# Slot experts of a ViT tower: a new queue order for the expert loads, a wait per part, and late fetches beside the last groups

## The chip, the cores and the metric

One core of a Trainium2 chip runs the whole kernel in one launch. The metric is the device time of that launch in microseconds (us), lower is better. The chip's other cores run nothing. The time before is the median of three runs; a profile of one further execution was taken by the hardware profiler.

## The reference

Input: 32 images of 96x96x3, cut into 36 patches of 16x16, plus a class token: 37 tokens of 192 per image. All arithmetic in the part that matters here is float32. Four stages follow each other, each with a residual and a layer norm:

1. low-rank attention with 12 heads;
2. a soft mixture of experts with 64 slots (the stage that is changed);
3. differential attention with 12 heads (two maps, `out1 - exp(lambda) * out2`), projected by `Wo`;
4. a segmented MLP with top-4 gates.

Stage 2, cut to what is computed:

```python
logits = einsum('sd,btd->bst', slot_directions, tokens)
dispatch_w = softmax(logits, axis=-1)
combine_w = softmax(logits, axis=-2)
y = einsum('btd,bst->bsd', xn, dispatch_w)               # 64 slot inputs per image
y = gelu(einsum('sio,bsi->bso', fc1_weight, y) + fc1_bias)   # 64 experts, 192 -> 768
y = einsum('sio,bsi->bso', fc2_weight, y) + fc2_bias         # 64 experts, 768 -> 192
out = einsum('bsd,bst->btd', y, combine_w)
```

Each of the 64 slots has its own two weight matrices, 192x768 and 768x192, so this stage reads 75 MB of weights, and each is used for 32 rows only.

## The kernel before

The kernel is written engine by engine. Each engine runs its own list of instructions in the order written, and waits for semaphores that others raise. There is no scheduler.

**Expert stage.** The 64 slots go in 16 groups of 4 (`GROUPS`, `GS`). A group needs `fc1` in three transfers: `fc1_tall` (128 partitions x 3072 words, 1536 KB), `fc1_short` (128 x 1536, 768 KB) and `fc1_b` (4 x 768, the bias, 12 KB); and `fc2` in two: 128 x 4608 words (2304 KB) and `fc2_b` (3 KB). All lie in one SBUF tile, `stream`, in two slots each (even and odd groups). The profile writes `fc1` and `fc2` alike as `in_fc_dram`.

**PE, `moe_pe` (L724).** `first(g)` makes the hidden layer of group g: 2 bias products (L728), 8 products with the tall part (L733), 8 with the short part (L739). A float32 product is two or more records in the trace, so that the counts there are twice these. Ahead of it stands one wait for 48 on `s_fc1`, which all three transfers of the group raise by 16 each; L733 also waits for the slot inputs that ACT stages (L775, L778). When `first(g)` is done, `s_hid` rises, and ACT applies gelu (L784). `second(g)` transposes the hidden layer (L747, 6), DVE copies it to SBUF (L799), PE adds the bias (L752) and makes 24 products with `fc2` (L757), and `s_fo` rises; DVE copies the result to `y_out` (L804) and raises `s_yo`. The order on PE is first(0), then first(1), second(0), first(2), second(1), first(3), second(2) and so on, to first(15), second(14), second(15).

**SP, `moe_sync` (L687).** SP issues the loads. Groups 0 and 1 are loaded during stage 1. Then a loop over pairs of groups, unrolled twice, in this order for each group g: wait until first(g-2) is done, issue the three transfers of fc1(g); wait until second(g-2) is done, issue fc2(g) and its bias; wait for `y_out`, store the 96 KB of group g-2 to `y_dram` (L689). Behind the loop come the stores of groups 14 and 15, the four weight matrices of stage 3 (L706, 864 KB together), and, when all stores have landed, the fetch of all slot outputs from `y_dram` into `y2` (L710, 2 transfers of 768 KB, in runs of 768 bytes). PE begins stage 3 (`l1_pe`, L898) when the four matrices and both halves of `y2` are there; its first products are those of L859.

**POOL, `split_pool` (L806),** works at the same time: it loads the first MLP weights, splits them into three bf16 parts and stores them (L822, L825).

Names that the change touches: `k_heads1` and the four late matrices share `stream` with the expert weights (L131, L133); `load_fc1` (L672), `moe_sync_first` (L681), `moe_sync` (L687), `first` (L725), the last three calls of `moe_pe` (L767 to L769), the wait at L899.

Of the kernel before, what the change touches and what calls it, by code (L numbers as in the profile page):

```python
# [22 lines left out]
SLOTS = 64  # L23
# [25 lines left out]
def tower(nc, io):  # L49
# [23 lines left out]
    with ExitStack() as ctx:  # L73
# [57 lines left out]
        k_heads1 = tenant(stream, FH, 0, [2, 2, QB, HH, T])  # L131
        w1s = tenant(stream, ZR, W1_AT, [SEG, SM * SH], bf16)
        late = Tenants(stream, KH * 2)  # L133
# [474 lines left out]
        s_fc1 = [sem("s_fc1_even"), sem("s_fc1_odd")]  # L608
        s_fc2 = [sem("s_fc2_even"), sem("s_fc2_odd")]
# [62 lines left out]
        def load_fc1(sp, u, g):  # L672


            w = io["fc1"][g]
            sp.dma_start(fc1_tall[:, u], w[0:64].rearrange("r k j h -> (r k) j h")).then_inc(s_fc1[u], 16)
            sp.dma_start(fc1_short[:, u],
                         w[64:FH].rearrange("r k (a j) h -> (r k a) j h", a=2)).then_inc(s_fc1[u], 16)
            sp.dma_start(fc1_b[:, u, :], w[FH:FH + 1, 0].rearrange("o j h -> (o j) h")).then_inc(s_fc1[u], 16)

        def moe_sync_first(sp):  # L681
            for g in range(2):
                load_fc1(sp, g, g)
                sp.dma_start(fc2[:, g], io["fc2"][g]).then_inc(s_fc2[g], 16)
                sp.dma_start(fc2_b[:, g, :], io["fc2_b"][g]).then_inc(s_fc2[g], 16)

        def moe_sync(sp):  # L687
            def store(g, u):
                sp.dma_start(y_dram.rearrange("s b d -> (s b) d")[ds(g * 128, 128), :], y_out[:, u, :]).then_inc(s_yd[u], 16)  # L689

            with sp.Fori(1, GROUPS // 2) as it:
                for u in range(2):

                    sp.wait_ge(s_hid, it * 2 + (u - 1))
                    load_fc1(sp, u, it * 2 + u)
                    sp.wait_ge(s_fo, it * 2 + (u - 1))
                    sp.dma_start(fc2[:, u], io["fc2"][it * 2 + u]).then_inc(s_fc2[u], 16)
                    sp.dma_start(fc2_b[:, u, :], io["fc2_b"][it * 2 + u]).then_inc(s_fc2[u], 16)
                    sp.wait_ge(s_yo, it * 2 + (u - 1))
                    store(it * 2 + (u - 2), u)  # L700
            for g in (GROUPS - 2, GROUPS - 1):
                sp.wait_ge(s_yo, g + 1)
                store(g, g % 2)

            for dst, name in ((w_q1, "w_q1"), (w_k1, "w_k1"), (w_v1, "w_v1"), (w_o1, "w_o1")):
                sp.dma_start(dst, io[name]).then_inc(s_late, 16)  # L706
            for u in range(2):
                sp.wait_ge(s_yd[u], 16 + 16 * (GROUPS // 2))
            for e in range(2):
                sp.dma_start(y2[64 * e:64 * e + SLOTS, :, :],  # L710
                             y_dram.rearrange("s (p e) d -> e s p d", e=2)[e]).then_inc(s_y2, 16)
# [12 lines left out]
        def moe_pe(pe):  # L724
            def first(it, u):  # L725
                pe.wait_ge(s_fc1[u], nth(it, 48, 48))
# [3 lines left out]
                pe.wait_ge(s_yr, nth(it, 6, 3 * u + 3))  # L730
                for n in range(2):
                    for j in range(GS):
                        pe.matmul(P[32 * j:32 * j + B, 2 * u + n, 0:HID // 2], tall_ring[:, u, B * j:B * (j + 1)],  # L733
                                  fc1_tall[:, u, j, n * (HID // 2):(n + 1) * (HID // 2)],
                                  start=False, stop=False, skip_group_check=True)
                for n in range(2):
# [25 lines left out]
            with pe.Fori(0, GROUPS // 2 - 1) as it:  # L762
# [3 lines left out]
                second(it, 1)  # L766
            first(GROUPS // 2 - 1, 1)  # L767
            second(GROUPS // 2 - 1, 0)
# [86 lines left out]
        def l1_pe(pe):  # L855
# [43 lines left out]
            pe.wait_ge(s_y2, 32)  # L899
# [904 lines left out]
```

## Time and profile before

| | |
|---|---|
| median of 3 runs | 1058.68 us (1057.67 to 1059.81) |
| the profiled execution, own time | 1055.97 us |
| its span in the profile | 1054.2 us |
| mean granted clock of TensorE | 0.819 of full |
| PE busy | 810.4 us (77%) |
| DVE busy | 562.6 us (53%) |
| ACT busy | 367.6 us (35%) |
| moved by DMA | 102.56 MB |
| transfers of expert weights on the chain of waits, by the page | 8% of the span |

The span is what the profiler saw of the program's work, so it is a little shorter than the execution's own time. The profile names instructions by line and tile: "L757 PE MATMUL P<-stream,work" is line 757 on PE, writing PSUM from `stream` and `work`. "SPq" is SP's queue issuing a transfer. The granted clock is a share of TensorE's full 2.4 GHz; 0.50 is 1.2 GHz. The DMA share is the mean busy share of the core's 16 DMA engines; since packets overlap it can read a little above 1.

### The profile page before, as it was taken

How to read it: one execution, taken by the hardware profiler on the slowest of the kernel's cores; microseconds unless marked ns; L12 is line 12 of the kernel's file. 1: busy time of each engine (PE TensorE's matmuls, PEld its weight loads, DVE VectorE, ACT ScalarE, POOL GpSimd, SP SyncE). 2: the span in 40 equal slices, each digit the busy share in tenths (PEclk: the TensorE clock that was granted, in tenths of full speed). 3: DMA queues.
4: the chain of work that ended last, by engine and by line, in shares of the span. 5: the costliest groups of instructions: out<-in, count | busy, mean ns of one | idle time of the engine just before them, and what ended most of it. 6: DMA issues, size and time to landing. Idle time of an engine off the chain costs nothing.

```text
span 1054.2 us, 19852 instructions
## 1 busy us (share of the span) xinstructions
PE 810.4 (77%) x6882; PEld 460.3 (44%) x6882; DVE 562.6 (53%) x1563; ACT 367.6 (35%) x785; POOL 98.4 (9%) x133
## 2 busy tenths in 40 slices
PE   6899999668677777729998897542799899899930
PEld 4567777553233333316766665211333333233310
DVE  4455656530000000025676867888587588677850
ACT  0313222203111111103334333233587587677700
POOL 0020201012322000000010110133000000000010
PEclk9786959558778788868898989665699999989975
DMA  8410000006999888686000000452200000000000
GB/s 311 188 36 1 35 0 0 1 1 218 373 387 405 338 354 356 270 160 84 1 2 1 0 1 1 139 80 44 60 2 1 2 1 1 2 1 1 1 13 23
DMA packets 24822, 102.56 MB, mean 97 GB/s; under 512 B 3359, under 2 KB 14563, under 8 KB 20531
## 3 DMA queue, kind: packets, MB, share of 16 engines
q1 hardware_dynamic: 23702, 98.37, 27.6%
q0 software_dynamic: 1056, 3.44, 1.0%
q8 instruction: 27, 0.44, 0.2%
q14 instruction: 37, 0.30, 0.1%
HBM read 93.08 MB, written 5.07 MB: 93 GB/s over the span
## 4 chain that ended last, share of the span: by engine, by line
PE 62%; DVE 14%; DMA 11%; issue 6%; SPq 2%; ACT 2%; POOL 1%; DVEq 0%; ACTq 0%; POOLq 0%
DMA stream<-in_fc_dram 8%; PE P L1440 7%; PE P L1415 7%; PE P L1424 7%; PE P L353 6%; PE P L1089 5%; PE P L415 4%; PE P L388 3%; PE P L399 3%; PE P L728 2%; PE P L733 2%; PE P L739 2%; PE P L757 2%; PE P L370 2%; PE P L1433 2%
## 5 line engine op out<-in xcount | busy, mean ns | idle before, releaser
L1584 DVE TENSOR_TENSOR work<-work,P 128x396 f32<-128x396 f32 x384 | 193.1, 562 | 65.3 <-PE P L1424 45.3
L1511 ACT ACTIVATE work<-P 128x396 f32<-128x396 f32 x384 | 178.5, 500 | 57.3 <-PE P L1415 56.9
L1415 PE MATMUL P<-stream 99*128 x384 | 129.4, 340 | 12.1 <-ACT work L1511 10.4
L1424 PE MATMUL P<-early,middle 96*128 x384 | 129.8, 339 | 0.6 <-DVE work L1584 0.6
L799 DVE COPY work<-P 128x768 f32<-128x768 f32 x16 | 15.3, 958 | 160.1 <-PE P L747 160.1
L1440 PE MATMUL P<-work 128*32 128x396 f32 x768 | 84.6, 508 | 0.0
L1415 PEld LDWEIGHTS P<-stream 99*128 99x128 bf16 x384 | 37.8, 98 | 100.5 <-ACT work L1511 54.2
L784 ACT ACTIVATE work<-P 128x768 f32<-128x768 f32 x16 | 13.0, 811 | 173.1 <-PE P L739 173.1
L728 PE MATMUL P<-stream,slot_sel 4*128 4x384 f32 x64 | 34.7, 676 | 47.3 <-DMA stream<-in_fc_dram 47.3
L584 POOL TENSOR_SCALAR work<-work 101x4 f32<-101x4 f32 x16 | 3.7, 229 | 700.0 <-DVE work L574 700.0
L1089 PE MATMUL P<-early 128*37 128x192 f32 x384 | 53.9, 361 | 10.1 <-DMA early<-in_patches_dram 7.1
L490 ACT ACTIVATE work<-work 101x444 f32<-101x444 f32 x48 | 28.1, 586 | 95.6 <-DVE work L485 95.6
L415 PE MATMUL P<-work 101*37 101x34 f32 x1152 | 53.9, 227 | 2.8 <-DVE work L474 2.8
L399 PE MATMUL P<-ident,work 101*128 101x101 f32 x288 | 44.5, 303 | 15.0 <-ACT work L490 12.5
L1424 PEld LDWEIGHTS P<-early,middle 96*128 96x128 bf16 x384 | 37.8, 98 | 35.4 <-DVE work L1584 17.4
L415 PEld LDWEIGHTS P<-work 101*37 101x37 f32 x1152 | 49.1, 142 | 9.5 <-issue 6.8
L1089 PEld LDWEIGHTS P<-early 128*37 128x37 f32 x384 | 37.0, 126 | 26.0 <-issue 10.5
L399 PEld LDWEIGHTS P<-ident,work 101*128 101x128 f32 x288 | 33.3, 169 | 34.2 <-issue 18.1
L353 PE MATMUL P<-work,stream 96*96 96x296 f32 x128 | 41.0, 484 | 4.1 <-DVE work L949 3.5
L757 PE MATMUL P<-stream,work 128*32 128x192 f32 x768 | 34.5, 328 | 8.5 <-DVE work L799 8.5
L457 DVE TENSOR_SCALAR stream<-P,hmask 96x296 f32<-96x296 f32 x48 | 21.5, 514 | 36.6 <-PE P L353 36.6
L480 DVE TENSOR_REDUCE work<-P 101x12 f32<-101x444 f32 x48 | 29.6, 616 | 21.0 <-PE P L388 20.7
(210 smaller groups left out, 1208.0 us busy)
## 6 DMA issues: line engine op xcount, KB each, us to landing
stream<-in_fc_dram SPq DMA_DIRECT2D x16, 2304.0 KB
stream<-in_fc_dram SPq DMA_DIRECT2D x16, 1536.0 KB
stream<-in_fc_dram SPq DMA_DIRECT2D x16, 768.0 KB
early<-stream SPq DMA_DIRECT2D x36, 99.0 KB, 2.3
early<-in_patches_dram SPq DMA_DIRECT2D x4, 888.0 KB, 5.1
stream<-w_dram SPq DMA_DIRECT2D x6, 512.0 KB
work<-in_w_dram SPq DMA_DIRECT2D x1, 2048.0 KB, 8.2
stream<-z_dram SPq DMA_DIRECT2D x6, 297.0 KB, 10.0
```

The costliest lines, as they stand in the source:

```text
L353: mm = pe.matmul(P[0:FH, at + mc, 0:QT], w[:, kc, m * D + mc * FH:m * D + (mc + 1) * FH], h_t[:, kc, :, :], start=(kc == 0), stop=(kc == 1))
L388: mm = pe.matmul(P[64 * e:64 * e + T, u % 2, mc * HH * T:(mc + 1) * HH * T], q_t[:, m, mc, b * T:(b + 1) * T], k_heads[:, m, mc, b, :, :], ...
L399: mm = pe.transpose(P[:, 4 + 2 * (u % 2) + hp // 3, (hp % 3) * ROWS:(hp % 3 + 1) * ROWS], probs[0:ROWS, u % 2, hp, :, :].rearrange("p a k ...
L415: mm = pe.matmul(P[64 * e:64 * e + T, 2 + u % 2, hp * w2:(hp + 1) * w2], probs_t[0:ROWS, u % 2, hp, 64 * e:64 * e + T], v_blk[0:ROWS, 2 * ...
L728: pe.matmul(P[:, 2 * u + n, 0:HID // 2], slot_sel[:, :], fc1_b[:, u, n * (HID // 2):(n + 1) * (HID // 2)], start=True, stop=False, skip_gr ...
L757: mm = pe.matmul(P[32 * j:32 * j + B, 6 + u, 0:D], hidden_t[:, u, c, B * j:B * (j + 1)], fc2[:, u, c, j, :], start=False, stop=(c == HC - ...
L1089: mm = pe.matmul(P[64 * e:64 * e + T, 2 + j // 2, (j % 2) * D:(j % 2 + 1) * D], patches[:, c, 2 * j + e, :], w_patch[:, c, :], start=(c == ...
L1415: pe.matmul(P[:, n % 3, 0:TC], w1s[:, seg, i * 128:(i + 1) * 128], zs[:, seg, ds(it * TC, TC)], start=True, stop=True).then_inc(s_u1, 1)
L1424: pe.matmul(P[:, 3 + n % 3, 0:TC], gate_sel[:, c, :], ws[:, 2 * seg + hh, ds(it * TC, TC)], start=True, stop=True).then_inc(s_bc, 1)
L1440: pe.matmul(P[32 * j:32 * j + 32, 6 + sq, 0:TC], w2[:, i, seg, :], gated[:, n % 8, :], start=False, stop=(hh == 1 and c == CH // 2 - 1), s ...
L1511: act.activation(act_out[:, n % 4, :], P[:, n % 3, 0:TC], ACT.Gelu_apprx_tanh).then_inc(s_ua, 1)
L1584: dve.tensor_tensor(gated[:, n % 8, :], act_out[:, n % 4, :], P[:, 3 + n % 3, 0:TC], ALU.mult).then_inc(s_ug, 1)
```

## The change

Four things:

1. SP issues each load when its own buffer comes free. `first(g-1)` ends on PE ahead of `second(g-2)`, so fc1(g+1) now stands ahead of fc2(g) in SP's list, where it stood behind it. The loop is written out (no registers). The store of a group moves with its fc2 step.
2. The bias parts are issued first of their group, and fc1's three transfers have a semaphore each; PE waits for each part just ahead of the products that read it.
3. PE's last three calls become second(14), first(15), second(15).
4. The four late matrices and `k_heads1` change places in `stream`, so that the matrices lie in the even slot of `fc1_tall`, free after first(14). They are issued behind fc2(15), with 12 of 16 groups' slot outputs (48 of 64 slots); the stores of groups 14 and 15 and a fetch of the last 16 slots follow. PE waits for four transfers of `y2` where it waited for two.

```diff
-        k_heads1 = tenant(stream, FH, 0, [2, 2, QB, HH, T])
+        k_heads1 = tenant(stream, FH, 12 * D, [2, 2, QB, HH, T])
...
-        late = Tenants(stream, KH * 2)
+        late = Tenants(stream)
...
             w = io["fc1"][g]
+            sp.dma_start(fc1_b[:, u, :], ...).then_inc(s_fc1_b[u], 16)
             sp.dma_start(fc1_tall[:, u], w[0:64]...).then_inc(s_fc1[u], 16)
-            sp.dma_start(fc1_short[:, u], ...).then_inc(s_fc1[u], 16)
-            sp.dma_start(fc1_b[:, u, :], ...).then_inc(s_fc1[u], 16)
+            sp.dma_start(fc1_short[:, u], ...).then_inc(s_fc1_short[u], 16)
+
+        def load_fc2(sp, u, g):
+            sp.dma_start(fc2_b[:, u, :], io["fc2_b"][g]).then_inc(s_fc2[u], 16)
+            sp.dma_start(fc2[:, u], io["fc2"][g]).then_inc(s_fc2[u], 16)
...
         def moe_sync(sp):
-            with sp.Fori(1, GROUPS // 2) as it:
-                for u in range(2):
-                    sp.wait_ge(s_hid, it * 2 + (u - 1))
-                    load_fc1(sp, u, it * 2 + u)
-                    sp.wait_ge(s_fo, it * 2 + (u - 1))
-                    sp.dma_start(fc2[:, u], ...).then_inc(s_fc2[u], 16)
-                    sp.dma_start(fc2_b[:, u, :], ...).then_inc(s_fc2[u], 16)
-                    sp.wait_ge(s_yo, it * 2 + (u - 1))
-                    store(it * 2 + (u - 2), u)
-            for g in (GROUPS - 2, GROUPS - 1):
-                sp.wait_ge(s_yo, g + 1)
-                store(g, g % 2)
+            def gather(groups, at, to):
+                for u in range(2):
+                    sp.wait_ge(s_yd[u], 16 + 16 * (groups // 2))
+                for e in range(2):
+                    sp.dma_start(y2[64 * e + at:64 * e + to, :, :],
+                                 y_dram.rearrange("s (p e) d -> e s p d", e=2)[e, at:to]).then_inc(s_y2, 16)
+
+            for g in range(2, GROUPS + 1):
+                if g < GROUPS:
+                    sp.wait_ge(s_hid, g - 1)
+                    load_fc1(sp, g % 2, g)
+                if g > 2:
+                    sp.wait_ge(s_fo, g - 2)
+                    load_fc2(sp, (g - 1) % 2, g - 1)
+                    store(g - 3)
+
+            sp.wait_ge(s_hid, GROUPS - 1)
             for dst, name in ((w_q1, "w_q1"), (w_k1, "w_k1"), (w_v1, "w_v1"), (w_o1, "w_o1")):
                 sp.dma_start(dst, io[name]).then_inc(s_late, 16)
-            for u in range(2):
-                sp.wait_ge(s_yd[u], 16 + 16 * (GROUPS // 2))
-            for e in range(2):
-                sp.dma_start(y2[64 * e:64 * e + SLOTS, :, :], ...).then_inc(s_y2, 16)
+            gather(GROUPS - 4, 0, SLOTS - 4 * GS)
+            for g in (GROUPS - 2, GROUPS - 1):
+                store(g)
+            gather(GROUPS, SLOTS - 4 * GS, SLOTS)
...
             def first(it, u):
-                pe.wait_ge(s_fc1[u], nth(it, 48, 48))
+                pe.wait_ge(s_fc1_b[u], nth(it, 16, 16))
...
                 pe.wait_ge(s_yr, nth(it, 6, 3 * u + 3))
+                pe.wait_ge(s_fc1[u], nth(it, 16, 16))
...
+                pe.wait_ge(s_fc1_short[u], nth(it, 16, 16))
...
+            second(GROUPS // 2 - 1, 0)
             first(GROUPS // 2 - 1, 1)
-            second(GROUPS // 2 - 1, 0)
             second(GROUPS // 2 - 1, 1)
...
-            pe.wait_ge(s_y2, 32)
+            pe.wait_ge(s_y2, 64)
```

SP's queue, one group of the loop (before). `in_fc1_dram` are the loads of fc1, `in_fc2_dram` of fc2; the ISA rows set up addresses from the loop's register:

```order
L676 ISA [waits s_hidden_made]
L676 DMA stream<-in_fc1_dram 128x3072
L677 ISA
L677 DMA stream<-in_fc1_dram 128x1536
L679 ISA
L679 DMA stream<-in_fc1_dram 4x768
L697 ISA [waits s_slots_out_made]
L697 DMA stream<-in_fc2_dram 128x4608
L698 ISA
L698 DMA fc2_b<-in_fc2_b_dram 4x192
L689 ISA [waits s_slots_out_taken]
L689 DMA y_dram<-work 128x192
```

And in the change, the same stretch (fc1 of group g, then fc2 of group g-1 and the store of group g-3):

```order
L678 DMA stream<-in_fc1_dram 4x768 [waits s_hidden_made]
L679 DMA stream<-in_fc1_dram 128x3072
L680 DMA stream<-in_fc1_dram 128x1536
L684 DMA fc2_b<-in_fc2_b_dram 4x192 [waits s_slots_out_made]
L685 DMA stream<-in_fc2_dram 128x4608
L695 DMA y_dram<-work 128x192 [waits s_slots_out_taken]
```

The kinds of rows are the same; the bias rows moved ahead of their group's large transfer. The groups shifted against each other too, which these rows don't show: the fc2 rows were those of the same group g as the fc1 rows above them, and are now those of group g-1.

SP's queue behind the last group (before):

```order
L689 DMA y_dram<-work 128x192 [waits s_slots_out_taken] x2
L706 DMA stream<-in_w_q1_dram 96x768
L706 DMA stream<-in_w_k1_dram 96x768
L706 DMA stream<-in_w_v1_dram 96x384
L706 DMA stream<-in_w_o1_dram 96x384
L710 DMA early<-y_dram 64x16x192 [waits s_slots_out_stored_odd,s_slots_out_stored_even]
L710 DMA early<-y_dram 64x16x192
```

And in the change, from fc2 of group 15 on:

```order
L685 DMA stream<-in_fc2_dram 128x4608
L695 DMA y_dram<-work 128x192 [waits s_slots_out_taken]
L717 DMA stream<-in_w_q1_dram 96x768 [waits s_hidden_made]
L717 DMA stream<-in_w_k1_dram 96x768
L717 DMA stream<-in_w_v1_dram 96x384
L717 DMA stream<-in_w_o1_dram 96x384
L702 DMA early<-y_dram 48x16x192 [waits s_slots_out_stored_odd,s_slots_out_stored_even]
L702 DMA early<-y_dram 48x16x192
L695 DMA y_dram<-work 128x192 [waits s_slots_out_taken] x2
L702 DMA early<-y_dram 16x16x192 [waits s_slots_out_stored_odd,s_slots_out_stored_even]
L702 DMA early<-y_dram 16x16x192
```

The matrices and the first fetch moved ahead of the last two stores, and a fetch of a quarter of the slots stands behind them.

PE, the last three calls in the change (before, the five rows of first(15), L728 to L739 there, stood ahead of the rows of second(14)):

```order
L759 MATMUL P<-ident,work 128x128 [waits s_hidden_active]
L759 MATMUL P<-ident,work 128x128 x5
L764 MATMUL P<-fc_b,slot_sel 128x192 [waits s_fc2_even]
L769 MATMUL P<-stream,work 32x192 [waits s_hidden_t]
L769 MATMUL P<-stream,work 32x192 x23
L738 MATMUL P<-stream,slot_sel 128x384 [waits s_fc1_bias_odd]
L738 MATMUL P<-stream,slot_sel 128x384
L744 MATMUL P<-stream,work 32x384 [waits s_fc1_odd,s_slot_inputs_staged]
L744 MATMUL P<-stream,work 32x384 x7
L751 MATMUL P<-stream,work 32x384 [waits s_fc1_short_odd]
L751 MATMUL P<-stream,work 32x384 x7
```

They show both edits on PE: second(14) went ahead of first(15), and the one wait at the head of `first` became three.

## Rows read from the trace of the kernel before

**Rows 1.** The page, 40 equal slices of the span: granted clock, DMA share in tenths.

```profile
PEclk9786959558778788868898989665699999989975
DMA  8410000006999888686000000452200000000000
```

**Rows 2.** Waits from 236 to 470 us: waiter, releaser, us in total, times, longest.

```profile
PE P L728 <- DMA stream<-in_fc_dram: 47.3, 11, 7.1
```

**Rows 3.** The chain of waits, one turn of two groups: start us, us, what.

```profile
380.23 2.92 PE P L728 x4
383.15 2.72 PE P L733 x16
385.87 2.56 PE P L739 x16
388.43 0.98 PE P L747 x6
389.43 0.97 DVE work L799
390.44 2.20 PE P L757 x48
392.80 0.33 SPq L697
...
395.79 11.79 DMA stream<-in_fc_dram
407.61 2.92 PE P L728 x4
```

**Rows 4.** Busy time by stretch: length, engines, then granted clock, DMA share, GB/s.

```profile
245.70:355.00 109.30, 78.09 (x739) 36.13 (x739) 10.52 (x16) 18.35 (x40) 25.30 (x36) 0.83 0.96 375
355.00:440.00 85.00, 61.48 (x570) 27.98 (x572) 7.89 (x12) 10.78 (x23) 0.00 (x0) 0.80 0.86 352
...
440.00:451.40 11.40, 10.23 (x132) 5.46 (x124) 2.31 (x4) 2.31 (x3) 0.00 (x0) 0.85 0.03 10
451.40:465.60 14.20, 0.01 (x1) 0.04 (x1) 0.32 (x1) 0.00 (x0) 0.00 (x0) 0.58 0.97 211
```

**Rows 5.** The same view, five shorter stretches of the expert stage.

```profile
265.00:275.00 10.00, 3.73 (x12) 1.55 (x16) 0.00 (x0) 0.00 (x0) 4.29 (x5) 0.71 1.00 426
...
396.00:416.00 20.00, 12.67 (x105) 5.29 (x98) 1.32 (x2) 1.59 (x5) 0.00 (x0) 0.74 1.00 422
423.00:438.00 15.00, 7.66 (x80) 3.99 (x76) 1.31 (x2) 0.81 (x1) 0.00 (x0) 0.84 1.01 428
249.60:264.20 14.60, 11.36 (x152) 6.37 (x148) 2.28 (x4) 4.24 (x9) 0.58 (x1) 1.00 0.94 331
271.20:279.40 8.20, 8.13 (x37) 2.54 (x37) 0.00 (x0) 0.00 (x0) 0.58 (x1) 0.50 0.98 411
```

**Rows 6.** PE in order of time: one `first` and one `second` at full clock.

```profile
255.84 1.55 PE L728 MATMUL P<-stream,slot_sel 4*128 4x384 f32 x4 [2.10 <-DMA stream<-in_fc_dram]
...
260.04 0.87 PE L747 MATMUL P<-ident,work 128*128 128x128 f32 x6
...
261.96 2.16 PE L757 MATMUL P<-stream,work 128*32 128x192 f32 x48 [0.53 <-DVE work L799]
```

**Rows 7.** In order of time: SP's first load of the stage, its fetch of `y2`, PE's next.

```profile
245.73 0.33 SPq L676 DMA_DIRECT2D stream<-in_fc_dram  x1
...
454.08 1.33 SPq L710 DMA_DIRECT2D early<-y_dram  x2
...
465.60 3.06 PE L859 MATMUL P<-early 128*101 128x192 f32 x8 [14.30 <-issue]
```

**Rows 8.** The chain of waits, the end of the late matrices and what follows.

```profile
453.54 4.73 DMA stream<-in_w_o_dram
458.27 7.32 issue
```

**Rows 9.** The page, transfers: KB each, us to landing.

```profile
stream<-in_fc_dram SPq DMA_DIRECT2D x16, 2304.0 KB
...
y_dram<-work SPq DMA_DIRECT2D x16, 96.0 KB, 8.9
```

More of the change, by code:

```diff
@@ L608, in tower @@
         s_fc1 = [sem("s_fc1_even"), sem("s_fc1_odd")]
+        s_fc1_b = [sem("s_fc1_bias_even"), sem("s_fc1_bias_odd")]
+        s_fc1_short = [sem("s_fc1_short_even"), sem("s_fc1_short_odd")]
         s_fc2 = [sem("s_fc2_even"), sem("s_fc2_odd")]
@@ L675, in load_fc1 @@
             w = io["fc1"][g]
+            sp.dma_start(fc1_b[:, u, :], w[FH:FH + 1, 0].rearrange("o j h -> (o j) h")).then_inc(s_fc1_b[u], 16)
             sp.dma_start(fc1_tall[:, u], w[0:64].rearrange("r k j h -> (r k) j h")).then_inc(s_fc1[u], 16)
             sp.dma_start(fc1_short[:, u],
-                         w[64:FH].rearrange("r k (a j) h -> (r k a) j h", a=2)).then_inc(s_fc1[u], 16)
-            sp.dma_start(fc1_b[:, u, :], w[FH:FH + 1, 0].rearrange("o j h -> (o j) h")).then_inc(s_fc1[u], 16)
+                         w[64:FH].rearrange("r k (a j) h -> (r k a) j h", a=2)).then_inc(s_fc1_short[u], 16)
+        def load_fc2(sp, u, g):
+            sp.dma_start(fc2_b[:, u, :], io["fc2_b"][g]).then_inc(s_fc2[u], 16)
+            sp.dma_start(fc2[:, u], io["fc2"][g]).then_inc(s_fc2[u], 16)
         def moe_sync_first(sp):
@@ L683, in moe_sync_first @@
                 load_fc1(sp, g, g)
-                sp.dma_start(fc2[:, g], io["fc2"][g]).then_inc(s_fc2[g], 16)
-                sp.dma_start(fc2_b[:, g, :], io["fc2_b"][g]).then_inc(s_fc2[g], 16)
+                load_fc2(sp, g, g)
         def moe_sync(sp):
-            def store(g, u):
-                sp.dma_start(y_dram.rearrange("s b d -> (s b) d")[ds(g * 128, 128), :], y_out[:, u, :]).then_inc(s_yd[u], 16)
-            with sp.Fori(1, GROUPS // 2) as it:
-                for u in range(2):
-                    sp.wait_ge(s_hid, it * 2 + (u - 1))
-                    load_fc1(sp, u, it * 2 + u)
-                    sp.wait_ge(s_fo, it * 2 + (u - 1))
-                    sp.dma_start(fc2[:, u], io["fc2"][it * 2 + u]).then_inc(s_fc2[u], 16)
-                    sp.dma_start(fc2_b[:, u, :], io["fc2_b"][it * 2 + u]).then_inc(s_fc2[u], 16)
-                    sp.wait_ge(s_yo, it * 2 + (u - 1))
-                    store(it * 2 + (u - 2), u)
@@ L701, in moe_sync, with store @@
-            for g in (GROUPS - 2, GROUPS - 1):
-                sp.wait_ge(s_yo, g + 1)
-                store(g, g % 2)
+            def store(g):
+                sp.wait_ge(s_yo, g + 1)
+                sp.dma_start(y_dram.rearrange("s b d -> (s b) d")[g * 128:(g + 1) * 128, :],
+                             y_out[:, g % 2, :]).then_inc(s_yd[g % 2], 16)
+            def gather(groups, at, to):
+                for u in range(2):
+                    sp.wait_ge(s_yd[u], 16 + 16 * (groups // 2))
+                for e in range(2):
+                    sp.dma_start(y2[64 * e + at:64 * e + to, :, :],
+                                 y_dram.rearrange("s (p e) d -> e s p d", e=2)[e, at:to]).then_inc(s_y2, 16)
@@ L709, in moe_sync @@
-            for e in range(2):
-                sp.dma_start(y2[64 * e:64 * e + SLOTS, :, :],
-                             y_dram.rearrange("s (p e) d -> e s p d", e=2)[e]).then_inc(s_y2, 16)
+            gather(GROUPS - 4, 0, SLOTS - 4 * GS)
+            for g in (GROUPS - 2, GROUPS - 1):
+                store(g)
+            gather(GROUPS, SLOTS - 4 * GS, SLOTS)
             for dst, name in ((z_proj, "z_proj"), (out1_w, "out1_w"), (out2_w, "out2_w"),
```

## The prediction

> **What bounds the kernel now.** I read the page first, for where the DMA engines work: slices 10 to 17 are the expert stage, and their share of 6 to 9 tenths says that they pause, and a clock row that goes up and down says that PE does too [rows 1]. The waits then say for whom that matters: PE waits 11 times for expert weights, 47.3 us in all [rows 2]. The chain of waits shows the loop that makes the pauses [rows 3]. One turn is two groups and takes 407.61 - 380.23 = 27.4 us: PE makes a `first` at half clock (8.2 us) and a `second` (4.2 us with DVE's copy); only when that ends may SP issue the fc2 and fc1 that stand next in its list (3.1 us until the last is out); they land 11.8 us later, and the next `first` starts. The transfer queue runs dry meanwhile, because fc1(g+1) stands behind fc2(g), although `first(g-1)` had freed its buffer one `second` earlier. The stretches put numbers to it [rows 4]: 375 GB/s at share 0.96 up to 355 us, 352 GB/s at 0.86 up to 440. Together 109.3 x 0.375 + 85 x 0.352 = 70.9 MB in 194.3 us, 365 GB/s. Where the queue never runs dry, 10 to 20 us at a time, it moves 422 to 428 GB/s [rows 5]. So the stage is bound by transfers with holes between them. Then comes a tail: DMA is at 0.03 from 440 to 451.4 us while PE works off groups 15 and 14, and PE idles from 451.4 to 465.6 us while the late matrices and the slot outputs come in, at 211 GB/s [rows 4].
>
> **The new order in SP's queue.** It adds no byte and no instruction that counts; it moves fc1(g+1) ahead of fc2(g). Is a load then always waiting? The queue's order becomes fc1(g+1), fc2(g), fc1(g+2), fc2(g+1), each 2.36 MB [rows 9], or 5.7 us at 412 GB/s. fc1(g+2) may be issued when first(g) ends, and first(g) can run as soon as fc1(g) is there, some 17 us before fc1(g+2) has to start. A `first` takes 4.2 us at full clock (255.84 to 260.04) and 8.2 at half; a `second` 4.1 (260.04 to 264.12) [rows 3, 6]. So PE may lag by 10 us or so before a hole appears: the queue stays full. From the first issue (245.73) [rows 7] plus about 1.3 us until bytes flow, 247, the 70.9 MB (POOL's traffic and the stores are in it) need 70.9 / rate. Bounds for the rate: 426 GB/s, a typical full stretch [rows 5], gives 166 us and an end at 413; the time that the engines were busy at all, 109.3 x 0.96 + 85 x 0.86 = 178 us, gives 425. The second counts the starts of bursts and the slow stretches beside POOL's stores (331 GB/s at share 0.94) [rows 5], of which the latter stay and the former mostly go. I take the middle, 412 GB/s: 172 us, end at T = 419. Before, the last weights landed at about 439 (DMA is down from 440 on [rows 4]). **Gain 20 us, between 14 and 26.**
>
> Nothing else pays for this: SP is held by its waits, not by issuing (6 issues of 0.3 to 0.5 us each in some 11.7 us per group). Each wait of SP (first(g-2), second(g-3), DVE's copy) is in the order in which PE gets to it, so nothing that could go stands behind a later wait.
>
> **A wait per part, biases first.** PE can do L728 (1.5 us at full clock) before the tall part lands and L733 before the short one. While transfers bound the stage, this only moves PE's work forward within a period in which PE idles anyway: nothing in the sum, at most 3 us once, at the last group. If the cover goes and PE becomes the bound, it costs nothing either, a passed wait being free.
>
> **The end.** fc2(15) lands at T, fc2(14) 5.7 us before. Behind T the queue still holds the matrices (0.88 MB) and three quarters of the slot outputs (1.18 MB). Before, the matrices, the slot outputs (1.57 MB) and a store took from 454.08 to 465.6; 2.06 MB at the 211 GB/s of that stretch [rows 4, 7] are 9.7 us, so the queue is clear at T + 9.7. PE meanwhile: second(14) ends at T - 3 (its fc2 lands at T - 5.7), first(15) at T + 1.2 at full clock or T + 5 at half. Now gelu of group 15 is exposed, about 1 us with its hand-over, since no `second` stands between; second(15) ends at T + 6.3 or T + 10.2; DVE's copy and the issue add 0.8. The last store goes out behind the fetch and lands 2 us after it: T + 12 to T + 13. The last fetch is 0.39 MB: of the 7.3 us that 1.57 MB took [rows 8], a quarter is 1.8, and I add 2 for issue and landing: PE starts L859 at T + 16, between 15 and 18. Before, it started at 465.6, that is 439 + 26.6 [rows 7]. **Gain 10.5 us, between 8.5 and 11.5.** PE starts stage 3 at half clock either way, as it now does (granted 0.58 in the idle stretch [rows 4]), so the stages behind only shift; the MLP weights that SP loads next have some 100 us of cover.
>
> **Sum.** 20 + 10.5 = 30.5 us, with bounds 22.5 and 37.5. The profiled execution took 1055.97 us, 2.7 less than the median; I take the same gain off the median: 1058.7 - 30.5 = 1028.2, say **1028 us**.
>
> **Rivals.**
>
> *A. The stream gets no faster.* The queue is fuller, but its mean rate stays at the 365 GB/s of before, since beside POOL's stores even a full queue moved 331 [rows 5]. Then the weights end at 247 + 70.9 / 0.365 = 441, and only the tail gains: 441 + 16 = 457 against 465.6, 8.6 us less, 1050 us. Against it: 45 us of full stretches at 422 to 428 GB/s [rows 5], two of the three without POOL. The Trainium skill ("DMA: Bandwidth & Descriptors", section "Where 436 GB/s comes from") has a rule that speaks against the change: for transfers from HBM a core is limited to about 358 GB/s. By it, an estimate, the weights end at 445 and the time is 1054 us. The trace disagrees, with the three stretches just named. Chance 0.08.
>
> *B. PE becomes the bound, and the kernel gets slower.* Now PE idles up to 7.1 us at a time [rows 2] and then works; the change cuts this into short waits ahead of each part. If the granted clock then stays at 0.5 (1.2 GHz), a `first` is 8.2 us [rows 3], and a `second` with its matmuls doubled is 1.7 + 1.0 + 4.4 = 7.1, an estimate. From 254 on PE has 14 `first` and 15 `second`: 14 x 8.2 + 15 x 7.1 = 221 us, to 475, plus 7 for copy, store and last fetch: 482, 16 later than now, about 1075 us. It decides from about 14 us per group on, against 11.7 of transfers. For it: half clock held through whole `first`s after such a wait (0.50 from 271.2 to 279.4) [rows 5]. Against it: from 249.6 to 264.2 us PE was busy 78% with waits of 0.5 to 2 us in between, as it would be now (8.3 of 11.7 is 71%), and was granted 1.00 [rows 5]; and a PE that is the bound doesn't wait. The skill ("TensorE: Matmul & The Clock Gate", section "HAM oscillation") says that waits for transfers between short groups of matmuls can throw the clock back in every group; the present trace does so once in two groups. At the mean clock of 0.82 now, PE needs about 10.8 us per group by these numbers, just under 11.7, so a few us of this is inside my range. Chance 0.04.
>
> *C. The tail gives little.* The late matrices and the first fetch stand ahead of the last two stores. If the stores land only well after them, or the last fetch, into 16 partitions, is as slow per transfer as the large one, L859 starts at T + 22 to T + 24: 1034 to 1036 us. For it: a store takes 8.9 us to land in the median, being behind loads [rows 9]. Chance 0.12.
>
> **Chances.** Forecast 0.74, C 0.12, A 0.08, B 0.04, anything else 0.02. The forecast with its bounds spans 1021 to 1036, with C up to 1036; with what the clock may add I take **1020 to 1040** as the range, which leaves out A, B and little more. About 0.2% is what a measurement of this kernel can tell from no change. All cases but B and a part of the rest are faster by far more: faster 0.94, the same 0.02, slower 0.04.
>
> **What the profile would show.** If right: DMA share at 0.97 or more and about 412 GB/s from 250 us to the landing of the last weights, no empty slice there; the wait of the bias products for weights nearly gone, and in its place short waits at the tall and short products; 14 groups at 11.7 us each; PE idle ahead of L859 for about 9 us, not 14.3; L859 at about 435. The MLP and output stages shifted and unchanged. Wrong if the share is near 1 and the rate under 390 (A), if PE has no idle time in the stage and a clock near 0.5 (B), or if the gap ahead of L859 is above 14 us (C).

## The result, and the profile after

The changed kernel took 1031.37 us (median of 4 runs, 1028.97 to 1035.84) against 1059.24 for the kernel before (median of 4): ratio 0.9734, 95% interval 0.9689 to 0.9778. A second measurement of the same kernel, with more runs on both sides (e5 below), gave 1029.06 against 1059.78, ratio 0.9700, 0.9677 to 0.9723. So the gain is 28 to 31 us by the medians. A ratio is not the quotient of the two medians beside it and can differ from it by some tenths of a per cent. The forecast was 1028 us, 30.5 less than before.

The profiled execution took 1035.84 us (span 1033.9), the slowest of its four; why is told below. The page of the changed kernel, the rows that answer to [rows 1] and the rate:

```profile
PEclk9787869657977787785799898665899999999975
DMA  8410100004999999890000001632100000000000
GB/s 308 201 37 1 35 0 0 1 1 182 418 429 422 401 424 424 187 110 4 1 2 1 0 1 68 108 60 47 48 2 2 2 1 1 2 1 1 1 14 23
```

From slice 11 on, the digits of DMA in the expert stage are now 9 but for one 8, where 9, 8 and 6 stood: the holes in the transfers are gone. The busy times by stretch of the changed kernel (length, engines, granted clock, DMA share, GB/s), answering to [rows 4]:

```profile
245.70:420.00 174.30, 141.01 (x1346) 68.99 (x1346) 19.71 (x30) 29.06 (x63) 25.12 (x35) 0.81 1.01 411
...
420.00:428.80 8.80, 7.32 (x92) 3.62 (x90) 0.97 (x2) 2.31 (x3) 0.00 (x0) 1.00 0.95 161
428.80:437.00 8.20, 0.00 (x0) 0.01 (x1) 0.36 (x1) 0.00 (x0) 0.00 (x0) 0.77 0.66 109
437.00:503.60 66.60, 60.54 (x456) 42.45 (x457) 35.17 (x101) 19.20 (x42) 3.03 (x5) 0.64 0.43 52
466.40:496.40 30.00, 30.00 (x264) 21.36 (x263) 18.52 (x59) 7.82 (x15) 1.27 (x2) 0.50 0.01 3
```

The first row is the forecast's core: 411 GB/s at share 1.01 until 420 us, where 365 GB/s stood until 440. 412 and 419 were predicted. The rate over the last 4 of these us is lower (229 to 301 GB/s, share 1.01 to 1.03), because the late transfers are already among them. The waits of the changed kernel from 236 to 450 us, answering to [rows 2]:

```profile
PE P L764 <- DMA stream<-in_fc_dram: 30.3, 10, 5.1
PE P L871 <- issue: 8.2, 1, 8.2
```

PE's wait for fc1 (L728 there, 47.3 us) is gone but for 0.2 us, twice, at the short products. What is left is a wait for fc2 ahead of L764 (10 times, 30.3 us): the load that PE needs next is simply the one that is landing. The page gives the depth of the queue, in us from issue to landing:

```profile
stream<-in_fc_dram SPq DMA_DIRECT2D x16, 1536.0 KB, 17.5
stream<-in_fc_dram SPq DMA_DIRECT2D x16, 768.0 KB, 19.0
```

At 5.7 us per 2.36 MB, 17 to 19 us is three loads deep. The end in order of time, PE and then SP's queue:

```profile
414.49 1.00 PE L764 MATMUL P<-fc_b,slot_sel 4*128 4x192 f32 x2 [5.06 <-DMA stream<-in_fc_dram]
415.43 4.07 PE L769 MATMUL P<-stream,work 128*32 128x192 f32 x48
419.42 1.62 PE L738 MATMUL P<-stream,slot_sel 4*128 4x384 f32 x4
...
424.69 0.88 PE L759 MATMUL P<-ident,work 128*128 128x128 f32 x6 [0.93 <-ACT work L796]
...
426.62 2.16 PE L769 MATMUL P<-stream,work 128*32 128x192 f32 x48 [0.53 <-DVE work L811]
437.02 3.06 PE L871 MATMUL P<-early 128*101 128x192 f32 x8 [8.24 <-issue]
```

```profile
408.33 0.33 SPq L685 DMA_DIRECT2D stream<-in_fc_dram  x1
...
411.18 7.75 SPq L702 DMA_DIRECT2D early<-y_dram  x2
420.04 9.53 SPq L695 DMA_DIRECT2D y_dram<-work  x2
431.09 1.22 SPq L702 DMA_DIRECT2D early<-y_dram  x2
```

fc2(14) lands at 414.4, second(14) ends at 419.5, first(15) at 423.8, second(15) at 428.8; the last store lands by 431.1, and the last fetch takes until 437.0. There the kernel is 465.6 - 437.0 = 28.6 us ahead of the kernel before [rows 7]. At the end of the span it is only 1054.2 - 1033.9 = 20.3 us ahead. The missing 8.3 us lie in one place, but for 0.1: from the first product of stage 3 to the first projection with `Wo` the kernel before took 58.4 us and this execution 66.6; the last row but one of the stretches shows it, and the last row shows that PE was granted 0.50 for 30 us of it while it was never idle. The kernel before had 0.78 over the whole of that stretch:

```profile
465.60:524.00 58.40, 49.77 (x457) 35.38 (x458) 34.59 (x101) 19.27 (x43) 3.03 (x5) 0.78 0.47 57
```

Two questions were left: is that loss part of the change, and which edit brought how much?

### The profile page after: what moved, and what is told of

Same layout as the page of the kernel before. It is cut to its first block, busy times and chain, and to the rows that moved or that the text cites. A ratio compares the mean times of both kernels' runs of the same rounds, so it can differ in the third digit from the quotient of the medians.

```text
span 1033.9 us, 19679 instructions
## 1 busy us (share of the span) xinstructions
PE 819.7 (79%) x6882; PEld 470.5 (46%) x6882; DVE 563.3 (54%) x1563; ACT 367.6 (36%) x785; POOL 98.4 (10%) x133
## 4 chain that ended last, share of the span: by engine, by line
PE 62%; DMA 13%; DVE 13%; issue 6%; ACT 2%; POOL 1%; SPq 1%; DVEq 0%; ACTq 0%; POOLq 0%
DMA stream<-in_fc_dram 11%; PE P L1452 8%; PE P L1427 7%; PE P L1436 7%; PE P L353 6%; PE P L1101 5%; PE P L415 5%; PE P L388 4%; PE P L399 4%; PE P L769 3%; PE P L370 2%; PE P L1445 2%; DVE work L1569 2%; DMA out_dram<-work 1%; PE P L1170 1%
## 5 line engine op out<-in xcount | busy, mean ns | idle before, releaser
L1427 PE MATMUL P<-stream 99*128 x384 | 129.5, 340 | 12.4 <-ACT work L1523 10.6
L415 PE MATMUL P<-work 101*37 101x34 f32 x1152 | 57.3, 233 | 2.3 <-DVE work L474 2.3
L399 PE MATMUL P<-ident,work 101*128 101x101 f32 x288 | 47.6, 319 | 13.0 <-ACT work L490 10.4
L415 PEld LDWEIGHTS P<-work 101*37 101x37 f32 x1152 | 52.4, 149 | 9.7 <-issue 7.6
L399 PEld LDWEIGHTS P<-ident,work 101*128 101x128 f32 x288 | 35.8, 179 | 33.6 <-issue 20.5
L769 PE MATMUL P<-stream,work 128*32 128x192 f32 x768 | 48.4, 419 | 3.2 <-DVE work L811 3.2
L816 DVE COPY work<-P 128x192 f32<-128x192 f32 x16 | 5.7, 358 | 77.7 <-PE P L769 77.7
L480 DVE TENSOR_REDUCE work<-P 101x12 f32<-101x444 f32 x48 | 29.6, 617 | 22.4 <-PE P L388 22.1
## 6 DMA issues: line engine op xcount, KB each, us to landing
stream<-in_fc_dram SPq DMA_DIRECT2D x16, 1536.0 KB, 17.5
```

The source lines that it names most:

```text
L399: mm = pe.transpose(P[:, 4 + 2 * (u % 2) + hp // 3, (hp % 3) * ROWS:(hp % 3 + 1) * ROWS], probs[0:ROWS, u % 2, hp, :, :].rearrange("p a k ...
L415: mm = pe.matmul(P[64 * e:64 * e + T, 2 + u % 2, hp * w2:(hp + 1) * w2], probs_t[0:ROWS, u % 2, hp, 64 * e:64 * e + T], v_blk[0:ROWS, 2 * ...
L480: dve.tensor_reduce(row_max[0:ROWS, u % 2, :], src, AX, ALU.max).then_inc(L["row_max"], 1)
L769: mm = pe.matmul(P[32 * j:32 * j + B, 6 + u, 0:D], hidden_t[:, u, c, B * j:B * (j + 1)], fc2[:, u, c, j, :], start=False, stop=(c == HC - ...
L1427: pe.matmul(P[:, n % 3, 0:TC], w1s[:, seg, i * 128:(i + 1) * 128], zs[:, seg, ds(it * TC, TC)], start=True, stop=True).then_inc(s_u1, 1)
```

## The experiments

"First product" below is the start of the first product of stage 3 (465.6 us before, 437.0 in the change), "stretch" the time from there to the first projection. Each profile is of one execution; ratios are against runs of the kernel before on the same chip.

### The order of the queue alone: e1 and e11

The kernel before with only this in `moe_sync` (biases last, one wait of 48, the old end):

```diff
-            with sp.Fori(1, GROUPS // 2) as it:
...
+            for g in range(2, GROUPS + 1):
+                if g < GROUPS:
+                    sp.wait_ge(s_hid, g - 1)
+                    load_fc1(sp, g % 2, g)
+                if g > 2:
+                    sp.wait_ge(s_fo, g - 2)
+                    sp.dma_start(fc2[:, (g - 1) % 2], io["fc2"][g - 1])...
```

> The kernel before with the new order of SP's queue alone (loop written out, fc1(g+1) ahead of fc2(g)); biases last, one wait of 48, PE's last calls, the late matrices and the fetch of the slot outputs as before. Theory 1 (steps overlap): the stream ends near 419 us as in the changed kernel, and since first(15) and second(14) are then done while fc2(15) is still landing, second(15) ends near 424 and the old tail of 14.2 us puts the first product of stage 3 near 438: 27 us less than before, ratio 0.974, almost the whole gain. Rival (the prediction's sum, 20 for the stream and 10.5 for the end, each on its own): first product near 446, ratio 0.981.

Measured: 1037.26 us (6 runs, 1026.98 to 1041.36), ratio 0.9786, 0.9738 to 0.9833. The profiled execution was its fastest, 1026.98 us. Its PE and SP near the end:

```profile
422.85 0.59 PE L753 MATMUL P<-fc_b,slot_sel 4*128 4x192 f32 x2 [2.49 <-DMA fc_b<-in_fc_b_dram]
423.37 3.79 PE L758 MATMUL P<-stream,work 128*32 128x192 f32 x48
441.27 3.05 PE L860 MATMUL P<-early 128*101 128x192 f32 x8 [14.12 <-issue]
```

The first product comes at 441.3: 24.3 us earlier than before by the order alone, more than the 20 that the prediction gave this step, less than the 27 of theory 1. Theory 1 had second(15) end near 424; here PE was released only at 422.85, by the bias of fc2(15), which lands behind it, then ran mostly at half clock and ended at 427.2, and the old tail of 14.1 us follows. The ratio lies between the two theories, and the spread of 14 us between runs of one kernel is wide. So it was run again.

> The kernel with the new order of SP's queue alone, a second time. The first time its profiled run took 1027.0 us and the five others 1031.5 to 1041.4. Theory (its trace): the first product of stage 3 comes 3 to 4 us later than in the changed kernel, and the rest of the spread is the granted clock at the start of stage 3: a median of 1032 to 1037, ratio 0.974 to 0.979. Rival (the end of the change is worth nothing): 0.970, as the changed kernel.

Measured: 1033.04 us (1029.53 to 1040.76), ratio 0.9786, 0.9736 to 0.9836, the same ratio, as theory had it. First product at 439.8, stretch 57.8. By the ratios the order alone is worth 22.7 us (2.14% of 1059) and the whole change 28 to 32; by the medians the order alone is worth 22.2 (e1) and 25.9 (e11) and the change 27.9 and 30.7. So the rest is worth some 2 to 9 us. The traces place 1.5 to 4.3 of them ahead of the first product (441.3 and 439.8 against 437.0 and 438.3), and part of that is the stream itself: counted from the moment when PE goes on with fc2(14), the first product comes 24.4 and 23.3 us later with the order alone, and 22.5 and 22.9 in the change. Where the others go no trace shows: the runs of e1 and e11 above 1035 us carry granted clocks of 0.805 to 0.816, those below 0.823 to 0.829, so the clock is a likely place, but none of the long ones was profiled, and two runs of e4 at 0.813 and 0.815 took only 1027.7 and 1027.8 us.

### The end alone: e2

The kernel before with the edits of the end only: places in `stream`, late matrices and first fetch ahead of the last two stores, second(14) ahead of first(15).

> The kernel before with the end alone changed: late matrices and 12 groups' slot outputs issued behind fc2(15), last fetch of 16 slots, PE's last calls second(14), first(15), second(15). Both theories: weights land near 439 as before, DMA share 0.86 from 355 to 440. second(14) is done before first(15)'s weights come at 435, first(15) to 443, gelu, second(15) to about 448, last fetch landed near 456: 9 to 10 us less than before, ratio 0.991. If the late transfers took bandwidth that the last weights need, the gain is under 6 us (0.995).

Measured: 1054.04 us (12 runs), ratio 0.9950, 0.9925 to 0.9976: 5.3 us, not 9 to 10, the number of the other branch (under 6 us), though the late transfers are not shown to have held up a load here. SP's queue at the end of its trace:

```profile
438.08 6.55 SPq L705 DMA_DIRECT2D early<-y_dram  x2
444.67 8.54 SPq L689 DMA_DIRECT2D y_dram<-work  x2
458.90 1.24 SPq L705 DMA_DIRECT2D early<-y_dram  x2
```

The last store is out at 453.2 and counts as landed at 458.9, 5.7 us later, and the last fetch of a quarter of the slots needs another 5.9 us. That is the mechanism of rival C, at work without the new order. In the changed kernel the queue has nearly drained when the last store goes out (429.6), and it lands in 1.5 us; the 5.9 us of the last fetch stay. In this execution the stage also began 2.7 us later and its loads came more slowly (355 GB/s up to 355 us, against 375), so that first(15) started at 441.5 and not at 435.0; the first product at 464.8 is only 0.8 us earlier than before. Counted from the start of first(15), it comes 23.3 us later and not 30.6: 7.3 us gained in this trace, where the runs have 5.3.

### The wait per part: e3

```diff
-                pe.wait_ge(s_fc1_b[u], nth(it, 16, 16))
+                pe.wait_ge(s_fc1[u], nth(it, 48, 48))
...
-                pe.wait_ge(s_fc1[u], nth(it, 16, 16))
...
-                pe.wait_ge(s_fc1_short[u], nth(it, 16, 16))
```

> The changed kernel with one wait of 48 ahead of the bias products in place of a wait per part. Theory 1: transfers bound the stage and PE waits at fc2, not at fc1, so nothing changes: ratio to before 0.973, stream end near 419. Rival (the wait per part carries part of the gain by keeping PE ahead): 2 us or more slower than the changed kernel, 0.976 or above.

Measured: 1027.90 us (1024.56 to 1030.88), ratio 0.9700, 0.9656 to 0.9744; first product at 439.5, stretch 54.4. No loss: the wait per part is worth nothing here. Unlike in the theory, PE then waits for both fc1 and fc2, 21.4 and 12.4 us, 33.8 together, in place of 30.3 at fc2 in the change (35.0 in its second profile): the wait moved and did not grow, as it should where transfers set the sum:

```profile
PE P L738 <- DMA stream<-in_fc_dram: 21.4, 10, 3.2
PE P L762 <- DMA stream<-in_fc_dram: 12.4, 6, 8.0
```

### first(15) ahead of second(14) again: e4

```diff
+            first(GROUPS // 2 - 1, 1)
             second(GROUPS // 2 - 1, 0)
-            first(GROUPS // 2 - 1, 1)
             second(GROUPS // 2 - 1, 1)
```

> The changed kernel with PE's last calls as before: first(15), second(14), second(15). Theory 1: in the changed kernel PE waited 5 us for fc2(14) with first(15)'s weights already there, so first(15) fits into that wait; second(15) ends near 424 and not 428.8, and the first product of stage 3 comes near 433 and not 437: 3 to 4 us faster than the changed kernel, ratio to before 0.970. Rival (the last store and fetch are held by the queue of late transfers, not by PE): first product at 437 still, 0.973.

Measured: 1027.76 us (1024.80 to 1030.03), ratio 0.9701, 0.9659 to 0.9743. The median fits theory 1, the trace does not: the first product comes at 439.3.

```profile
426.20 1.00 PE L764 MATMUL P<-fc_b,slot_sel 4*128 4x192 f32 x2 [4.26 <-DMA stream<-in_fc_dram]
427.13 4.07 PE L769 MATMUL P<-stream,work 128*32 128x192 f32 x48
439.28 3.05 PE L871 MATMUL P<-early 128*101 128x192 f32 x8 [8.08 <-issue]
```

PE did fit first(15) into its wait, and was then held by fc2(15) itself, which landed only at 426.2. The rival was right that PE's order is not what holds the end, but the queue holds it through fc2(15), not through the last store. In the change, PE's later order hides that landing: it comes to fc2(15) at 425.5 and finds it there. And this execution was 2.3 us behind the change's when PE went on with fc2(14) (416.8 against 414.5); from there to the first product both took 22.4 to 22.5 us. PE's last calls may stand either way.

### The change again, and PE kept busy: e5 and e6

> The changed kernel as it is, a second time, beside the others. Its first profile lost 8.2 us from the first product of stage 3 (437.0) to the first projection (503.6, 66.6 us; 58.4 in the kernel before), all at a granted clock of 0.50 from 466 to 496 us. Theory (the clock's level there is a matter of the moment, not of the change): this profile shows 54 to 58 us for that stretch and a time near 1026, the median of all stays near 1030 with a spread of 6 us or more. Rival (the change sets the low clock): 64 us or more again.

Measured: 1029.06 us (6 runs, 1027.30 to 1031.07). First product at 438.3, and the stretch:

```profile
438.30:496.90 58.60, 49.97 (x456) 35.48 (x457) 34.60 (x101) 19.23 (x42) 3.03 (x5) 0.78 0.49 58
```

58.6 us at 0.78, as before the change. The rival falls: the 8 us that the first profile gave back belong to that execution and not to the change. Of the theory the stretch is near, the rest is not: this profile took 1029.05 us, not 1026, and the six runs spread by 3.8 us, not 6. For e6, idle products were put where PE waits:

```diff
+            def keep_busy(n):
+                for _ in range(n):
+                    pe.matmul(P[:, 0, 0:384], ident[:, :], cw...[:, 0:384], start=True, stop=True, ...)
+
+            keep_busy(9)
             pe.wait_ge(s_late, 64)
...
+            keep_busy(5)
             pe_turn(pe, L1, 0, h_in, L0["h_out"], QP, QUADS)
```

> The changed kernel with 9 idle products (128x384 of ident and cw into a free PSUM bank) on PE between second(15) and the first product of stage 3, and 5 more ahead of the first transposes, where PE waits for transfers and for DVE and POOL. Theory: the waits there leave stage 3 at half clock (its first q and k products took 10.2 us); kept busy, PE starts at full clock: that stretch from first product to first projection falls to about 50 us in every run, ratio to before about 0.966 (5 to 8 us off the changed kernel) and a smaller spread. Rival (the clock there follows something else, or the added products delay the first one): stretch of 54 us or more, ratio 0.971 or above.

Measured: 1024.60 us (1019.77 to 1028.24), ratio 0.9647, 0.9622 to 0.9673, against 1029.06 for the change beside it: 4.5 us less. The stretch is 55.5 us at 0.88:

```profile
440.00:495.50 55.50, 49.89 (x467) 35.26 (x468) 34.45 (x101) 19.30 (x43) 3.03 (x5) 0.88 0.52 62
```

The gain in the runs is clear (the intervals of the two ratios don't meet); the forecast of about 50 us for the stretch was too good, and the runs spread by 8.5 us, more than the change's. Where the 4.5 us come from this profile can't tell: it is of the slowest of the six runs (1028.24 us, 0.8 less than the change's profile), and its first product came 1.7 us later than there, so that of the 3.1 us that the stretch is shorter 1.4 are left at its end. Nor does the stretch's mean clock single out the idle products, since kernels without them had the same 0.88 and a shorter stretch (e1, e3 and e4, 54.4 us each). The row of e3:

```profile
439.50:493.90 54.40, 44.68 (x457) 31.46 (x458) 34.32 (x101) 19.29 (x43) 3.04 (x5) 0.88 0.52 63
```

What parts the profiles without idle products is a spell at half clock late in the stretch: the last 18.6 us of e5 had 0.72, the last 14.4 of e3 1.00. What the idle products do show is at the entry. The first q and k products took 10.1 to 11.6 us without them, 9.9 in e6 and 8.2 in e9 below. The Trainium skill ("TensorE: Matmul & The Clock Gate", section "HAM oscillation") says that waits for transfers between short groups of matmuls can throw the clock back. The rows agree for the entry to stage 3: over the 8.6 us from the first product on, the granted clock was 0.50 in e5, 1.00 in e6 and 0.65 in e9. So the gain of 4.5 us is measured, and the clock at the entry as its cause is in part argued. What the page's rule does not explain is 0.50 for 30 us without one idle microsecond, as in the first profile of the change.

### Direct copies at the end: e7

One wait of 48, first(15) first, and for groups 12 to 15 two copies from `y_out` straight into `y2`, with no last fetch:

```diff
+                if g >= GROUPS - 4:
+                    for e, s in ((0, s_yd), (1, s_yx)):
+                        sp.dma_start(y2[64 * e + g * GS:64 * e + (g + 1) * GS, :, :],
+                                     y_out[e:128:2, g % 2, :]).then_inc(s[g % 2], 16)
+                    return
```

> The changed kernel with one wait of 48 per group, first(15) ahead of second(14), and groups 12 to 15 copied from y_out straight into y2 (SBUF to SBUF, two transfers of 48 KB per group) in place of store, landing and last fetch. Theory: behind second(15) stand the last store (1.5 us to landing), the issue and 5.9 us of last fetch; a direct copy needs about 3 us in their place, so PE's wait ahead of stage 3 falls from 8.2 to 3 to 4 us and the first product comes near 433 to 434: 5 us off, ratio to before 0.966. Rival (the queue of late matrices and of the first fetch is what holds it): wait of 7 us or more, ratio 0.970.

Measured: 1029.78 us, ratio 0.9701, 0.9677 to 0.9726: no gain.

```profile
429.13 1.00 PE L765 MATMUL P<-fc_b,slot_sel 4*128 4x192 f32 x2 [5.81 <-DMA stream<-in_fc_dram]
430.06 4.07 PE L770 MATMUL P<-stream,work 128*32 128x192 f32 x48
440.09 3.06 PE L878 MATMUL P<-early 128*101 128x192 f32 x8 [5.96 <-DMA early<-work]
```

PE's wait ahead of stage 3 did shrink, from 8.2 to 6.0 us (3 to 4 were forecast, with a direct copy at about 3 us), but fc2(15) landed at 429.1, 3 us later than in e4. Both theories missed that: by this trace, what stands in the queue with fc2(15) delays it, and what was saved behind it was lost ahead of it.

### Half of fc2: e8

```diff
-            sp.dma_start(fc2[:, u], io["fc2"][g]).then_inc(s_fc2[u], 16)
+            part = HC if g < 2 else HC // 2
+            sp.dma_start(fc2[:, u, 0:part], io["fc2"][g][:, 0:part]).then_inc(s_fc2[u], 16)
```

> The changed kernel with only half of fc2 (its first 3 of 6 parts) loaded for groups 2 to 15; products unchanged, so the output of these groups uses old weights. 14 x 1.18 MB = 16.5 MB less. Theory (transfers bound the stage at 411 GB/s): the first product of stage 3 moves from 437 to 397 if nothing else binds; PE needs 8.3 us per group at full clock and up to 10.8 at the mean clock, against 8.6 for transfers, so PE takes over in part: 397 to 412, 25 to 40 us less. Rival (PE's chain sets the pace already): under 10 us less.

Measured, one run: 995.42 us, 34 to 36 less than the change; first product at 405.2, inside the forecast and 32 to 33 us earlier than in the two profiles of the change. At 411 GB/s, 16.5 MB are 40 us; four fifths of that came. In its first stretch the engines still moved 403 GB/s at share 1.00, and PE was granted 0.98:

```profile
245.70:355.00 109.30, 94.91 (x1076) 47.22 (x1076) 15.43 (x23) 26.94 (x58) 24.60 (x34) 0.98 1.00 403
```

Transfers bound the changed stage. PE made a group every 9.6 us here (ten groups from 276.15 to 372.22), at full clock, where the change's took 12.2 (twelve from 268.52 to 414.49); it still waited up to 1.1 us per group, and the 8.6 us of the forecast, which left POOL's traffic and the stores out, was not reached. This is the strongest evidence against rival B.

### Late transfers held back until fc2(15) has landed: e10

```diff
             sp.wait_ge(s_hid, GROUPS - 1)
+            sp.wait_ge(s_fc2[1], 32 * (GROUPS // 2))
```

(with first(15) ahead of second(14), as e4)

> The changed kernel with first(15) ahead of second(14), and SP waiting until fc2(15) has landed before it issues the late matrices and the first fetch. With them right behind, fc2(15) landed at 426.2 us (PE waited for it at the bias product); with nothing behind it, in the kernel with the order alone, PE went on at 422.85. Theory (transfers queued behind it slow fc2(15) down): it lands at 422 to 424 here, and second(15) ends near 427 to 428; but the late transfers then need 10 us of their own, with the last store behind them, and the first product of stage 3 comes at 440 to 444, no earlier than the 439.3 of before. Rival (a strict first-in first-out): it lands at 426 again.

Measured, one run: 1032.44 us.

```profile
423.42 0.59 PE L765 MATMUL P<-fc_b,slot_sel 4*128 4x192 f32 x2 [0.55 <-DMA stream<-in_fc_dram]
423.94 2.16 PE L770 MATMUL P<-stream,work 128*32 128x192 f32 x48
443.72 3.06 PE L872 MATMUL P<-early 128*101 128x192 f32 x8 [17.63 <-issue]
```

fc2(15) was there at 423.4 and not at 426.2, as theory had it, though it was issued 0.9 us later than in e4 (409.29 against 408.35): what is queued behind a load slows it. The other traces bear this out. From the moment when the last part of fc1(15) let PE go on, fc2(15) took 11.3 us here and 11.6 and 11.4 in e1 and e11, all with no late transfer behind it; with them it took 15.0 in e4 and 14.7 in e9, and 18.2 in e7. And the first product comes 4.4 us later than in e4, since the late transfers lie bare. Queuing them early is right, and costs about 3 us at fc2(15).

### The version that looks best: e9

PE kept busy, one wait per group, first(15) ahead of second(14).

> The version that looks best: the changed kernel with PE kept busy ahead of stage 3, one wait of 48 per group and first(15) ahead of second(14). Theory: the busy products are worth 4 to 5 us (1024.6 against 1029.1 beside each other), the other two edits nothing to 2 us: 1022 to 1025 us, ratio 0.964. Rival (the busy products' gain was the moment's clock): 0.968 or above.

Measured: 1024.37 us (1022.99 to 1027.98), ratio 0.9687, 0.9644 to 0.9730. The median is as expected, the ratio is not: 0.964 was forecast, 0.968 or above is the rival's, and the interval covers both. It is wide, since the runs of before scattered from 1050.8 to 1064.8 here. First product at 438.3, stretch 53.8, the shortest of all; fc2(15) had let PE go on at 424.67:

```profile
438.30:492.10 53.80, 49.14 (x467) 35.28 (x468) 34.41 (x101) 19.29 (x43) 3.03 (x5) 0.88 0.53 63
```

It does not differ from e6 (1024.60). Both medians lie 4.5 us or more below the change's, though only e6 was timed beside the change. That the gain is that of the busy products is the likely reading; e3 and e4, whose other edits it has, stand at 1027.9 and 1027.8, against 1029 to 1031 for the change: 1 to 3 us that their intervals don't separate from nothing.

## Why the prediction was right, point by point

**The stream (20 us predicted).** Right in mechanism and size. Predicted: 412 GB/s and an end at 419. Measured: 411 GB/s up to 420 (e5: 411 up to 355 us, then 421 up to 415). With the order alone (e1, e11) the transfers fall off at 419, before at 439: 20 us. The middle between the rate of full stretches and the busy time fitted, as POOL's traffic stayed in and the burst starts went. The groups came every 12.2 us where 11.7 were forecast; the 11.7 left POOL's traffic out, which the 70.9 MB of the sum have in. The buffer argument held as well: loads wait three deep, 17.5 us from issue to landing, and from 250 to 415 us the DMA share of no 5 us fell under 0.95.

One reading of it was wrong and did no harm. The prediction lets fc2(15) land at T = 419, with the late transfers behind it. They take their share before it is in: PE could go on with it at 424.7 and 426.2 where it waited for it behind such a queue (e9, e4), and at 423.4 with nothing behind it. In the change PE comes to it at 425.5, as second(14) and first(15) still stand ahead, so the landing is hidden; fc2(14), the last load that held PE, was there at 414.4, and 413.3 was forecast.

**The wait per part (0 predicted).** Right in size (e3), wrong in where PE would wait. The prediction expected short waits at the tall and short products; the trace has 0.2 us twice there and 30.3 us at fc2's bias. PE's order is first(g+1), second(g), and the queue's is fc1(g+1), fc2(g): when PE gets to second(g), fc2(g) is what is landing.

**The end (10.5 us predicted).** Here the prediction's split was wrong, and the sum right. Its step "PE starts L859 at T + 16, before at 439 + 26.6" took the 26.6 us behind the last landing as the price of the old end. But 12.4 of them were PE working off first(15), second(14) and second(15), which had piled up behind the last burst. With the queue full and the old last calls, PE has done all but second(15) when fc2(15) lands: with the order alone, the first product came at 441.3 and 439.8, 24 to 26 us earlier. So the order brought 24 to 26 us ahead of stage 3, not 20, and the end 1.5 to 4.3, not 10.5. The sum is no luck all the same, since it rests on a schedule from T to the first product, and that came 2 to 3 us late only. Had only the end been changed, 9 to 10 us were forecast (e2) and 5.3 came. The price of the last fetch was too low: 5.9 us with its issue, where a quarter of 7.3 plus 2 was taken (3.8).

**Ahead of stage 3:** 435 predicted, 437.0 and 438.3 measured; of the 2 to 3 us, 2 are that fetch.

**Sum.** 30.5 us predicted; 27.9 in the first measurement and 30.7 in the second.

**The rivals.** A (the stream gets no faster) fell by the rate. The Trainium skill's limit of about 358 GB/s for transfers from HBM ("DMA: Bandwidth & Descriptors", section "Where 436 GB/s comes from") does not hold here: one core moved 411 GB/s for 174 us. B fell by the change's own trace (PE waited 30.3 us for transfers, at a mean clock of 0.81) and by e8: PE at 0.98 while busy 87% with short waits. Of C, the late landing of the last store happened in e2, and in the change only the slow last fetch did.

**What the prediction had no term for:** the granted clock behind the change. It said that the later stages only shift. They do in most executions, but a single one can lose 8 us there, and the one profiled did. The stretch at the head of stage 3 took 53.8 to 58.7 us in the profile before and in all eleven of the experiments, and 66.6 in this one.

## What to carry to other kernels

When a queue runs dry although two buffers exist, look at which buffer comes free first and whether the list of loads has that order: 22 to 26 of these some 30 us needed no new buffer, byte or semaphore. Price such a change from the rate in stretches where the queue never ran dry, with the traffic of others in it (here 411 GB/s beside POOL's and 421 without), and do not add a second term for work that had only piled up behind the last burst. Transfers queued right behind the last load hide their own time, but take some of that load's. And time it by many runs: a single profile of this kernel can be 8 us off through the clock alone.

## What the runs showed of the hardware that was not expected

- A load is slowed by what is queued behind it on the same queue: fc2(15), issued at 408.4, was there at 426.2 with 2 MB of late transfers behind it (1.2 MB of them the fetch in runs of 768 bytes), and at 423.4, issued at 409.3, with none; with the direct copies around it, at 429.1. All came from SP's one queue.
- A store of 96 KB counts as landed 1.5 us after its issue behind a nearly empty queue (429.6 to 431.1) and 5.7 us behind a busy one (453.2 to 458.9).
- A busy PE can be held at half clock: from 466.4 to 496.4 us in the changed kernel's first profile it was busy for all of 30 us and granted 0.50. No other profile has a spell of that length in this stretch; shorter ones close the stretch in e5 and before (0.62 over the last 8.6 us of e5, PE busy throughout), and e1, e3 and e4 have none there. What sets it stays open.
